# A routed-expert stage with 17 tiles of 256 slots and 6 of 128 in place of 23 tiles of 256

## The chip, the cores and the metric

The kernel runs on one core of a Trainium2 chip. The metric is the device time of the whole program in microseconds (us), the median of several runs. Engines are named as in the profile: PE is TensorE (matmuls), PEld its weight loads, DVE is VectorE, ACT is ScalarE, POOL is GpSimd, SP is SyncE, which here only issues transfers.

## What is computed

A decoder layer on x of 4 x 512 rows of 512 numbers: a gated recurrence, a cross attention, and a block of self attention and experts, with a layer norm behind each of the three. The change touches only the experts. There are 8 routed experts of inner width 352 and a shared expert of inner width 1408; each of the 2048 rows goes to the two routed experts with the largest router probability:

```python
top_w, top_i = jax.lax.top_k(probabilities, 2)        # of 8 experts, for each row
g = jnp.einsum('th,ehi->eti', h, w_gate_e)            # 512 -> 352
u = jnp.einsum('th,ehi->eti', h, w_up_e)              # 512 -> 352
y = jnp.einsum('eti,eih->eth', jax.nn.silu(g) * u, w_down_e)
routed = jnp.einsum('eth,te->th', y, combine)         # combine: the two weights of a row
sh = jax.nn.silu(h @ w_sh_gate) * (h @ w_sh_up) @ w_sh_down
x = x + routed + sh * jax.nn.sigmoid(h @ w_sh_eg)
```

## The kernel before

The last part of the program, moe (from L1959), runs as a list of passes (schedule, L1946): 12 passes of the shared expert (six parts of its width, two row groups each), then 23 passes of the routed experts, one for each tile, then 12 more of the shared expert. A tile (class Pass, L1936) is TW = 256 places for rows of one expert; there are NTILES = 23 of them, enough for any split of the 4096 pairs of row and expert. Which expert a tile belongs to is found on the chip: places (in the VectorE block) counts the rows of each expert, gives every pair of row and expert a slot, and fills the row numbers up_row and dn_row with which GpSimd later picks an expert's weights by indirect transfers.

Every product is made of three matmuls with the operands split into a high and a low part (product3, L132). In a routed tile the weights are stationary (128 of the 352 inner columns at a time, the last chunk has 96) and 256 rows move: three chunks, each 12 matmuls for gate and 12 for up. So the activation comes out with the inner width on the partitions, as the down product needs it. The down product (down, L2504) makes 128 rows at a time: the activation is stationary, 512 output columns move, 9 matmuls.

TensorE's order in a routed pass p is: gate and up of chunk 0; the down product of pass p - 1; gate of chunk 1; the turning of the next tile's rows (turn, L2482: 8 transposes from hs); up of chunk 1; chunk 2. The wait for the low parts of the rows (s_tlo) stands ahead of each pass, and the wait for the loaded rows (s_hs) in turn. ScalarE takes the sigmoid (L2233), the high part of the activation (L2240), the high parts of the next tile's gate and up weights (split_up, L2194, two of 128 x 1408), the high parts of the next tile's rows (high_rows, L2214), the high part of this tile's down weights (split_down, L2203) and the results (L2259). VectorE does the gating (L2293, L2296) and the low parts of all of them (L2278, L2282, L2301, L2400).

The raw weights have one landing buffer each (up_raw, dn_raw): GpSimd issues the transfer for the next tile (pick_up L2153, pick_down L2161) when VectorE has split the last. The split gate and up weights have two buffers, the rows hs two, the results ys four. SyncE works through one list: for each tile it issues the load of the rows of the tile after next (load_rows, L2082), then waits for and issues the stores of this tile's results (store_rows, L2088). So a load of rows stands behind the stores of the tile two before it, and these wait for ScalarE's results.

## Time and profile before

| what | us |
| --- | --- |
| median of 3 runs (2492.18 to 2497.55) | 2493.06 |
| the profiled execution | 2495.78 |
| its span | 2494.1 |
| TensorE busy in the span | 2374.0 |
| VectorE busy | 1353.1 |
| ScalarE busy | 1351.2 |
| GpSimd busy | 927.6 |

The span is what the profile's times count from and cover; the profiled execution's own time is 1.7 us longer. The routed passes lie between about 1976 and 2290 us of the span. In the views an instruction is given with the line of the kernel, what it writes and what it reads; matmuls overlap, so the duration of a single one is longer than their distance, and the chain of waits, which gives each matmul the time by which it moved the end, is the place to read a matmul's price.

### The profile page before, as it was taken

How to read it: one execution, taken by the hardware profiler on the slowest of the kernel's cores; microseconds unless marked ns; L12 is line 12 of the kernel's file. 1: busy time of each engine (PE TensorE's matmuls, PEld its weight loads, DVE VectorE, ACT ScalarE, POOL GpSimd, SP SyncE). 2: the span in 40 equal slices, each digit the busy share in tenths (PEclk: the TensorE clock that was granted, in tenths of full speed). 3: DMA queues.
4: the chain of work that ended last, by engine and by line, in shares of the span. 5: the costliest groups of instructions: out<-in, count | busy, mean ns of one | idle time of the engine just before them, and what ended most of it. 6: DMA issues, size and time to landing. Idle time of an engine off the chain costs nothing. (4 is left out here: it accounts for less than half of the span.)

```text
span 2494.1 us, 39149 instructions
## 1 busy us (share of the span) xinstructions
PE 2374.0 (95%) x15376; PEld 1537.8 (62%) x15376; DVE 1353.1 (54%) x2105; ACT 1351.2 (54%) x1714; POOL 927.6 (37%) x610
## 2 busy tenths in 40 slices
PE   8999899999999999999998899998899999999997
PEld 6877444444444444444334556565588899999885
DVE  6676534434443434443413755555565677776785
ACT  4332577677766777667995443433422366665221
POOL 1237654565465535654212433332033021221320
PEclk9999899999999999999999999999899999999999
DMA  6003774667455764756745000001144277775430
GB/s 219 17 18 106 221 197 117 157 167 194 118 146 158 196 170 97 186 155 167 191 87 203 18 1 18 1 18 54 60 163 160 92 238 243 243 237 185 144 119 34
DMA packets 206935, 331.46 MB, mean 133 GB/s; under 512 B 71264, under 2 KB 125792, under 8 KB 206560
## 3 DMA queue, kind: packets, MB, share of 16 engines
q1 hardware_dynamic: 188256, 252.80, 35.8%
q0 software_dynamic: 16336, 72.23, 8.8%
q10 hardware_dynamic: 2160, 3.93, 0.5%
q8 instruction: 122, 2.00, 0.3%
q14 instruction: 61, 0.50, 0.1%
HBM read 241.53 MB, written 99.42 MB: 137 GB/s over the span
## 5 line engine op out<-in xcount | busy, mean ns | idle before, releaser
L1052 ACT ACTIVATE A_c_prob<-c_psum 128x1024 f32<-128x1024 f32 x832 | 786.8, 1029 | 277.4 <-PE c_psum L1302 271.3
L982 POOL TENSOR_TENSOR E_c_roots<-E_c_roots,c_half 128x32 f32<-128x32 f32 (+1 forms) x70 | 363.3, 5191 | 406.6 <-DVE E_c_roots L1069 406.5
L1311 PE MATMUL c_psum<-A_c_prob,c_vq 128*17 128x512 f32 x3328 | 415.4, 599 | 8.6 <-DVE c_oT L1204 8.3
L137 PE MATMUL c_psum<-E_c_w,E_c_c 128*128 128x512 f32 x1248 | 313.8, 401 | 3.1 <-DVEq L1189 2.2
L1302 PE MATMUL c_psum<-c_qq,c_kq 64*128 64x512 f32 x1664 | 287.9, 438 | 18.8 <-ACT A_c_prob L1052 11.3
L137 PEld LDWEIGHTS c_psum<-E_c_w,E_c_c 128*128 128x128 f32 x1248 | 227.4, 188 | 124.6 <-issue 41.0
L1302 PEld LDWEIGHTS c_psum<-c_qq,c_kq 64*128 64x128 f32 x1664 | 136.6, 185 | 167.2 <-ACT A_c_prob L1052 91.4
L1108 DVE COPY E_c_unit<-c_psum 128x256 f32<-128x256 f32 x89 | 37.8, 425 | 327.8 <-PE c_psum L137 327.8
L2504 PE MATMUL m_psum<-A_m_dn_hi,A_m_a 128*128 128x512 f32 (+1 forms) x628 | 204.3, 394 | 2.2 <-DVE A_m_a L2301 2.2
L137 PE MATMUL m_psum<-R_m_t,m_up_hi 128*128 128x256 f32 (+1 forms) x1104 | 200.0, 283 | 0.0
L1311 PEld LDWEIGHTS c_psum<-A_c_prob,c_vq 128*17 128x17 f32 x3328 | 68.6, 96 | 188.4 <-issue 163.7
L1742 DVE TENSOR_REDUCE s_topx<-s_psum 128x4 f32<-128x2048 f32 (+1 forms) x64 | 95.5, 1492 | 146.2 <-PE s_psum L1860 137.0
L137 PEld LDWEIGHTS m_psum<-R_m_t,m_up_hi 128*128 128x128 f32 (+1 forms) x1104 | 165.8, 179 | 2.1
L2240 ACT ACTIVATE A_m_a<-Q_m_work 128x256 fp32r<-128x256 f32 (+2 forms) x113 | 56.7, 502 | 200.9 <-DVE Q_m_work L2296 159.2
L137 PE MATMUL m_psum<-R_m_t,m_up_lo 128*128 128x256 f32 (+1 forms) x552 | 154.7, 280 | 0.0
L1653 ACT ACTIVATE A_s_pT<-s_psum 128x2048 f32<-128x2048 f32 (+1 forms) x64 | 79.5, 1242 | 121.2 <-PE s_psum L1874 120.9
L2504 PEld LDWEIGHTS m_psum<-A_m_dn_hi,A_m_a 128*128 128x128 f32 (+1 forms) x628 | 117.8, 188 | 28.6 <-DVE A_m_a L2301 2.7
L137 PE MATMUL r_psum<-E_x,E_w_hi 128*128 128x512 f32 x384 | 121.0, 397 | 10.0 <-DVE E_w_lo L414 9.2
L2233 ACT ACTIVATE Q_m_work<-m_psum 128x256 f32<-128x256 f32 (+2 forms) x113 | 51.9, 459 | 134.2 <-PE m_psum L137 134.2
L2504 PE MATMUL m_psum<-Q_m_dn_lo,A_m_a 128*128 128x512 f32 (+1 forms) x314 | 123.1, 392 | 0.0
L975 POOL TENSOR_TENSOR E_c_c<-E_c_raw,E_c_c 128x512 fp32r<-128x512 f32 x89 | 118.7, 1333 | 7.1
L137 PE MATMUL m_psum<-R_g_hi,m_up_hi 128*128 128x512 f32 x264 | 105.6, 400 | 3.6 <-DVE m_up_lo L2278 3.6
(316 smaller groups left out, 4216.7 us busy)
## 6 DMA issues: line engine op xcount, KB each, us to landing
c_kq<-kd SPq DMA_DIRECT2D x248, 208.0 KB, 6.1
kd<-S_c_t SPq DMA_DIRECT2D x96, 256.0 KB, 4.0
E_c_raw<-in_ctxT SPq DMA_DIRECT2D x89, 256.0 KB, 4.2
qd<-A_c_q SPq DMA_DIRECT2D x64, 256.0 KB
c_qq<-qd SPq DMA_DIRECT2D x64, 256.0 KB, 3.1
vd<-A_c_vt SPq DMA_DIRECT2D x104, 136.0 KB, 3.0
c_vq<-vd SPq DMA_DIRECT2D x31, 442.0 KB, 9.0
R_m_hs<-slots SPq DMA_DIRECT2D x23, 512.0 KB
```

The costliest lines, as they stand in the source:

```text
L137: mm = pe.matmul(out, a(c), b(c), start=first and i == 0, stop=last and i == len(terms) - 1)
L975: pool.tensor_tensor(c_lo[:, job % 2], c_raw[:, n % CB], c_hi[:, job % 2], ALU.subtract).then_inc(s_clo, 1)
L982: pool.tensor_tensor(rr[:, unit % RB, 0:n], ms[:, unit % RB, 0:n], half[:, 0:n], ALU.pow).then_inc(s_r, 1)
L1052: act.activation(prob[:, t % PB, 2 * (u % 2):2 * (u % 2) + 2, :], score_banks[u % 3], ACT.Exp, scale=XD ** -0.5).then_inc(s_ex, 1)
L1108: dve.tensor_copy(raw[:, unit % RB, at:at + HD], src[:, 0:HD]).then_inc(s_k, 1)
L1302: mm = pe.matmul(score_banks[u % 3][:, s, :], kq[rows, q % 2, u % 2, kt * P:(kt + 1) * P], qq[rows, q % 2, u % 2, :], start=True, stop=True)
L1311: mm = pe.matmul(o_bank[32 * j:32 * j + VW, :], vq[:, q % 2, kt, j, :], prob[:, t % PB, j, :], start=kt == 0, stop=kt == CT - 1)
L1653: act.activation(pT[:, kt % 2, :, 0:L], psum[:, 0:HPC, 0:L], ACT.Exp, scale=SCALE).then_inc(s_ex, 1)
L1742: dve.reduce_max(topx[:, t, ::SD], psum[:, 0:HPC, 0:(t + 1) * P], AX_X).then_inc(s_top, 1)
L2233: act.activation(sig[0:rows, 0:width], gu_bank[n % 2][0][0:rows, 0:width], ACT.Sigmoid).then_inc(s_sig, 1)
L2240: act.activation(a_hi[0:rows, p % 2, i, 0:width], act_f[0:rows, 0:width], ACT.Copy).then_inc(s_ahi, 1)
L2504: mm = pe.matmul(y_bank[t], a[0:rows, p % 2, i, ts], w[0:rows, i, :], start=k == 0, stop=k == 3 * len(x.chunks) - 1)
```

## The change

Six of the 23 tiles become tiles of 128 slots; their places in the order are after the 3rd, 6th, 9th, 12th, 15th and 17th tile of 256 (ORDER). An expert's rows are cut into as many tiles of 256 as they fill by more than half of the last, and its last 128 or fewer go to a short tile; if the short tiles are used up or not needed, tiles of 256 or empty ones stand in, which places works out with a longer list of small VectorE operations. In a short tile (Pass.turned) the rows are stationary and the weights move, 352 columns at a time: 12 matmuls for gate and 12 for up. The activation then has the rows on the partitions, so three transposes on TensorE turn it, into the bank in which the gate product was, and ScalarE and VectorE take its high and low part from there. TensorE's order in a short tile is: gate; turn of the next tile's rows; up; the down product of the pass before; the three transposes. ScalarE's is: sigmoid, first weight split, rows, second weight split, down weights, results of the pass before, turned activation. VectorE's is: first half of the gating, first weight split, second half, second weight split, rows, down weights, low part of the turned activation. Loads, stores and turns of a short tile handle one block of 128 rows in place of two.

```diff
-NTILES = (B * T * 2 - NEXP) // TW + NEXP
-SLOTS = NTILES * TW
+PAIRS, SINGLES = 17, 6
+HALVES = 2 * PAIRS + SINGLES
+NTILES = PAIRS + SINGLES
+SLOTS = HALVES * P
+
+
+def order_of_tiles():
+
+    out, pair = [], 0
+    for single in range(SINGLES):
+        upto = min(3 * single + 3, PAIRS)
+        out += [*range(pair, upto), PAIRS + single]
+        pair = upto
+    return out
+
+
+ORDER = order_of_tiles()
+first_half = lambda column: 2 * column if column < PAIRS else column + PAIRS
...
-        self.subs = TT if self.shared else TW // P
-        self.chunks = [(i * P, P) for i in range(CHUNKS[unit_of(stage)])] if self.shared else IT
+        self.subs = TT if self.shared else 1 + (ORDER[tile] < PAIRS)
+        self.width = self.subs * P
+        self.turned = self.subs == 1
+        self.inner = [(i * P, P) for i in range(CHUNKS[unit_of(stage)])] if self.shared else IT
+        self.chunks = [(0, P)] if self.turned else self.inner
+        self.across = MI if self.turned else self.width
...
-                rows = slots[tile * TW:(tile + 1) * TW].rearrange("(s p) n -> p s n", p=P)
-                sp.dma_start(hs[:, tile % 2], rows).then_inc(s_hs[tile % 2], 16)
+                at, subs = first_half(ORDER[tile]), passes[R0 + tile].subs
+                rows = slots[at * P:(at + subs) * P].rearrange("(s p) n -> p s n", p=P)
+                sp.dma_start(hs[:, tile % 2, 0:subs], rows).then_inc(s_hs[tile % 2], 16)
 
             def store_rows(tile):
-                for s in range(TW // P):
-                    n = tile * (TW // P) + s
+                for s in range(passes[R0 + tile].subs):
+                    n, at = esub(R0 + tile) + s, first_half(ORDER[tile]) + s
                     sp.wait_ge(s_ye, n + 1)
-                    sp.dma_start(yslots[n * P:(n + 1) * P], ys[:, n % NY]).then_inc(s_ys[n % NY], 16)
+                    sp.dma_start(yslots[at * P:(at + 1) * P], ys[:, n % NY]).then_inc(s_ys[n % NY], 16)
...
+                def high_turned():
+                    act.wait_ge(s_turned, turned_before(p) + 1)
+                    act.wait_ge(s_y, ysub(p - 1))
+                    act.activation(a_hi[:, p % 2, :, 0:P], gu_bank[base(p) % 2][0][:, 0:NI * P].rearrange("p (i n) -> p i n", i=NI), ACT.Copy).then_inc(s_ahi, 1)
...
+                if x.turned:
+                    sigmoid(0)
+                    split_up(w + 1, 0)
+                    if not passes[p + 1].shared:
+                        high_rows(passes[p + 1].tile)
+                    split_up(w + 1, 1)
+                    split_down(w)
+                    results()
+                    high_turned()
+                    continue
...
+            def low_turned(x):
+                n = base(x.p)
+                dve.wait_ge(s_ahi, n + 1)
+                dve.tensor_tensor(a_lo[:, x.p % 2, :, 0:P], gu_bank[n % 2][0][:, 0:NI * P].rearrange("p (i n) -> p i n", i=NI),
+                                  a_hi[:, x.p % 2, :, 0:P], ALU.subtract).then_inc(s_alo, 1)
...
-                own.done(dve.tensor_reduce(many[:], few, AX_X, ALU.add))
+                each = lambda ap: ap.unsqueeze(2).to_broadcast([P, NEXP, NTILE])
+                per_tile = lambda ap: ap.unsqueeze(1).to_broadcast([P, NTILES, NEXP])
+                halves = count_f[:].unsqueeze(2).to_broadcast([P, NTILES, NEXP])
+                placed = by_expert(place[:])
+                behind = few_f
+                own.done(dve.tensor_scalar(below, ranks_f[:, 0:NEXP], -float(NEXP), None, ALU.add))
+                own.done(dve.tensor_reduce(np_e, few[:, :, 1::2], AX_X, ALU.add))
+                own.done(dve.tensor_reduce(ns_e, few[:, :, 0::2], AX_X, ALU.add))
                 own.wait()
-                own.done(dve.tensor_tensor_scan(upto_e[:], ones[:, 0:NEXP], many[:], 0.0, ALU.mult, ALU.add))
+                own.done(dve.tensor_tensor(ns_e, ns_e, np_e, ALU.subtract))
+                own.done(dve.tensor_tensor_scan(pairs_e, ones[:, 0:NEXP], np_e, 0.0, ALU.mult, ALU.add))
                 own.wait()
-                own.done(dve.tensor_tensor(many[:], upto_e[:], many[:], ALU.subtract))
+                own.done(dve.tensor_tensor_scan(singles_e, ones[:, 0:NEXP], ns_e, 0.0, ALU.mult, ALU.add))
+                own.done(dve.tensor_tensor(pair_at, pairs_e, np_e, ALU.subtract))
                 own.wait()
-                own.done(dve.scalar_tensor_tensor(by_expert(place[:]), many[:].unsqueeze(2).to_broadcast([P, NEXP, NTILE]), float(TW), by_expert(place[:]), ALU.mult, ALU.add))
-                own.done(dve.tensor_tensor(compared, upto_e[:].unsqueeze(1).to_broadcast([P, NTILES, NEXP]),
-                                           count_f[:].unsqueeze(2).to_broadcast([P, NTILES, NEXP]), ALU.is_le))
+                pairs = pairs_e[:, NEXP - 1:NEXP]
+                own.done(dve.scalar_tensor_tensor(turn_e, singles_e, pairs, ns_e, ALU.add, ALU.subtract))
+                own.wait()
+                own.done(dve.tensor_scalar(single_at, turn_e, float(PAIRS), pairs, ALU.min, ALU.max))
+                own.wait()
+                own.done(dve.tensor_tensor(single_at, single_at, turn_e, ALU.add))
+                own.wait()
+                own.done(dve.scalar_tensor_tensor(shift, pairs_e, -2.0, single_at, ALU.mult, ALU.add))
+                own.done(dve.scalar_tensor_tensor(by_expert(behind), each(np_e), float(TW), placed, ALU.mult, ALU.is_le))
+                own.done(dve.tensor_tensor(ns_e, ns_e, below, ALU.mult))
+                own.wait()
+                own.done(dve.tensor_tensor(by_expert(behind), by_expert(behind), each(shift), ALU.mult))
+                own.done(dve.scalar_tensor_tensor(placed, each(pair_at), float(TW), placed, ALU.mult, ALU.add))
+                own.done(dve.scalar_tensor_tensor(compared, per_tile(pairs_e), 2.0, halves, ALU.mult, ALU.is_le))
+                own.done(dve.tensor_tensor(matched, per_tile(single_at), halves, ALU.is_equal))
+                own.wait()
+                own.done(dve.scalar_tensor_tensor(place[:], behind, float(P), place[:], ALU.mult, ALU.add))
+                own.done(dve.tensor_tensor(matched, matched, per_tile(ns_e), ALU.mult))
+                own.wait()
+                own.done(dve.tensor_tensor(compared, compared, matched, ALU.add))
...
+                if x.turned:
+                    gated(x, 0, 0)
+                    split_up(w + 1, 0)
+                    gated(x, 0, 1)
+                    split_up(w + 1, 1)
+                    if not passes[p + 1].shared:
+                        low_rows(passes[p + 1].tile)
+                    split_down(w)
+                    low_turned(x)
+                    continue
...
+                if x.turned:
+                    n = base(p)
+                    pe.wait_ge(s_a, n - 1)
+                    for j in range(2):
+                        product3(pe, gu_bank[n % 2][j][:, 0:MI], lambda c: hi[:, c, 0:P], lambda c: lo[:, c, 0:P],
+                                 lambda c: up_hi[:, w % 2, j, c, :], lambda c: up_lo[:, w % 2, j, c, :], KC).then_inc(s_gu, 1)
+                        if j == 0 and not passes[p + 1].shared:
+                            turn(passes[p + 1].tile)
+                    down(passes[p - 1])
+                    pe.wait_ge(s_a, n + 1)
+                    for i in range(NI):
+                        mm = pe.transpose(gu_bank[n % 2][0][:, i * P:(i + 1) * P], act_f[:, i * P:(i + 1) * P], ident[:])
+                    mm.then_inc(s_turned, 1)
+                    continue
...
                         pe.wait_ge(s_a, n - 1)
+                        if n - 2 in turned_chunks:
+                            pe.wait_ge(s_alo, n - 1)
```

The rest gives the short tiles their widths and counts in the same functions, issues one more iota, and takes the buffers of the new small operations from places that are free at that time.

## Rows read from the trace of the kernel before

**Rows 1.** View by windows, twenty routed tiles (us, then each engine's busy us, PEclk, DMA share, GB/s)

```profile
2000.73:2273.52 272.79, 272.79 (x1962) 257.04 (x1962) 201.35 (x320) 173.33 (x301) 55.24 (x58) 1.00 0.71 241
```

**Rows 2.** Chain of waits in order of time: start us, us, what, how many

```profile
2081.67 0.88 PE m_psum L2482 x8
2082.55 7.10 PE m_psum L137 x60
2089.65 4.24 PE m_psum L2504 x18
...
2300.22 11.14 PE m_psum L137 x48
```

**Rows 3.** Timeline of ScalarE, one routed pass and a shared one: start us, us, instruction

```profile
1808.00 0.58 ACT L2233 ACTIVATE Q_m_work<-m_psum 128x512 f32<-128x512 f32 x1
...
2102.49 0.36 ACT L2233 ACTIVATE Q_m_work<-m_psum 128x256 f32<-128x256 f32 x1
2102.75 1.37 ACT L2194 ACTIVATE m_up_hi<-S_up_raw 128x1408 fp32r<-128x1408 f32 x1
...
2105.63 0.58 ACT L2259 ACTIVATE R_m_ys<-m_psum 128x512 f32<-128x512 f32 x1
...
2109.50 1.57 ACT L2214 ACTIVATE R_m_t<-m_psum,S_w 128x256 fp32r<-128x256 f32 x4
2110.94 1.51 ACT L2203 ACTIVATE A_m_dn_hi<-Q_m_dn_raw 128x1536 fp32r<-128x1536 f32 x1
```

**Rows 4.** Timeline of VectorE in the same routed pass

```profile
2103.13 0.42 DVE L2293 TENSOR_TENSOR Q_m_work<-m_psum,Q_m_work 128x256 f32<-128x256 f32 x1
...
2104.16 1.62 DVE L2278 TENSOR_TENSOR m_up_lo<-S_up_raw,m_up_hi 128x1408 fp32r<-128x1408 f32 x1 [0.15 <-ACT m_up_hi L2194]
...
2110.37 1.66 DVE L2400 SCALAR_TENSOR_TENSOR R_m_t<-m_psum,S_w,R_m_t 128x256 fp32r<-128x256 f32 x4 [2.67 <-ACT R_m_t L2214]
...
2112.74 1.75 DVE L2282 TENSOR_TENSOR Q_m_dn_lo<-Q_m_dn_raw,A_m_dn_hi 128x1536 fp32r<-128x1536 f32 x1
```

**Rows 5.** Timeline of SyncE's queue in a routed pass

```profile
2092.60 2.27 SPq L2088 DMA_DIRECT2D yslots<-R_m_ys  x2
...
2094.91 0.43 SPq L2082 DMA_DIRECT2D R_m_hs<-slots  x1
```

**Rows 6.** DMA view, 2101-2102, 2102-2103: packets, MB, share; then landing of seven stores

```profile
q1 hardware_dynamic: 57, 0.10, 27.1%
...
q1 hardware_dynamic: 8, 0.01, 3.7%
...
DMA to landing us min/median/max: 4.2/4.7/5.4
```

**Rows 7.** View by windows, while weights, results and rows are all under way

```profile
2093.50:2100.45 6.95, 6.95 (x60) 6.91 (x59) 4.27 (x8) 4.62 (x9) 0.94 (x1) 1.00 0.94 312
```

**Rows 8.** View by windows, two stops of TensorE, the second with what follows it

```profile
210.13:212.33 2.20, 0.00 (x1) 0.01 (x1) 0.00 (x0) 0.60 (x1) 0.41 (x4) 1.00 0.00 0
213.70:217.20 3.50, 3.50 (x12) 2.72 (x11) 0.10 (x1) 0.51 (x1) 3.50 (x1) 0.51 0.76 285
226.03:231.00 4.97, 3.38 (x17) 2.57 (x16) 4.87 (x10) 2.98 (x4) 4.74 (x1) 1.00 0.26 88
```

**Rows 9.** Timelines around places, TensorE's chain there, and GpSimd's later wait

```profile
1814.59 0.21 DVE L2354 TENSOR_REDUCE m_many<-S_m_equal 128x8 f32<-128x64 f32 x1
...
1818.74 0.18 DVE L2380 CAST m_slot<-S_m_slot 128x32 int32<-128x32 f32 x1
...
1826.16 0.69 DVE L2296 TENSOR_TENSOR Q_m_work<-Q_m_work,m_psum 128x512 f32<-128x512 f32 x1 [1.17 <-PE m_psum L137]
1827.55 0.69 DVE L2301 TENSOR_TENSOR A_m_a<-Q_m_work,A_m_a 128x512 fp32r<-128x512 f32 x1 [0.70 <-ACT A_m_a L2240]
...
1831.62 5.48 PE m_psum L2504 x24
...
1950.52 1.15 POOL L2153 DMA_INDIRECT S_up_raw<-in_up,m_up_row  x1 [30.93 <-DVE m_up_lo L2278]
```

More of the change, by code:

```diff
@@ L1972, in moe @@
     base = lambda p: sum(len(x.chunks) for x in passes[:p])
+    turned_before = lambda p: sum(x.turned for x in passes[:p])
+    turned_chunks = {base(x.p) for x in passes if x.turned}
     routed = lambda w: unit_of(w) is None
@@ L2020, in moe @@
         rank = S.tile("m_rank", at_s + NEXP * NTILE, NTILE, NEXP)
-        many = m.sb("many", [P, NEXP])
-        upto_e = m.sb("upto_e", [P, NEXP])
+        np_e, ns_e, pairs_e, singles_e, pair_at, turn_e, single_at, shift, below = (restart[:, i * NEXP:(i + 1) * NEXP] for i in range(9))
         picked = m.sb("picked", [P, NTILE, NEXP])
@@ L2224, in _ @@
                 p, w = x.p, x.stage
-                width = T if x.shared else TW
+                width = x.across
                 prev = passes[p - 1] if p else None
@@ L2240, in high_act, with results @@
                     act.activation(a_hi[0:rows, p % 2, i, 0:width], act_f[0:rows, 0:width], ACT.Copy).then_inc(s_ahi, 1)
+                def high_turned():
+                    act.wait_ge(s_turned, turned_before(p) + 1)
+                    act.wait_ge(s_y, ysub(p - 1))
+                    act.activation(a_hi[:, p % 2, :, 0:P], gu_bank[base(p) % 2][0][:, 0:NI * P].rearrange("p (i n) -> p i n", i=NI), ACT.Copy).then_inc(s_ahi, 1)
+                def results():
+                    for s in range(prev.subs):
+                        n = esub(p - 1) + s
+                        act.wait_ge(s_y, ysub(p - 1) + s + 1)
+                        if n >= NY:
+                            act.wait_ge(s_ys[n % NY], 16 * (n // NY))
+                        act.activation(ys[:, n % NY], y_bank[s], ACT.Copy).then_inc(s_ye, 1)
                 fresh = first[w] == p and w + 1 < stages
                 single = len(x.chunks) == 1
+                if x.turned:
[8 more added lines that the diff above has]
+                    continue
                 sigmoid(0)
@@ L2253, in _ @@
                 if prev and not prev.shared:
-                    for s in range(prev.subs):
-                        n = esub(p - 1) + s
-                        act.wait_ge(s_y, ysub(p - 1) + s + 1)
-                        if n >= NY:
-                            act.wait_ge(s_ys[n % NY], 16 * (n // NY))
-                        act.activation(ys[:, n % NY], y_bank[s], ACT.Copy).then_inc(s_ye, 1)
+                    results()
                 if first[w] == p and w and x.shared:
@@ L2285, in _, with gated @@
                 split_up(0, j)
-            def gated(x, i):
-                n, rows, width = base(x.p) + i, x.chunks[i][1], T if x.shared else TW
-                dve.wait_ge(s_sig, n + 1)
-                if n:
-                    dve.wait_ge(s_alo, n)
-                    dve.wait_ge(s_ahi, n)
-                dve.tensor_tensor(act_f[0:rows, 0:width], gu_bank[n % 2][0][0:rows, 0:width], sig[0:rows, 0:width], ALU.mult).then_inc(s_t1, 1)
+            def gated(x, i, half=None):
+                n, rows, width = base(x.p) + i, x.chunks[i][1], x.across
+                if half != 1:
+                    dve.wait_ge(s_sig, n + 1)
+                    if n:
+                        dve.wait_ge(s_alo, n)
+                        dve.wait_ge(s_ahi, n)
+                    dve.tensor_tensor(act_f[0:rows, 0:width], gu_bank[n % 2][0][0:rows, 0:width], sig[0:rows, 0:width], ALU.mult).then_inc(s_t1, 1)
+                if half == 0:
+                    return
                 dve.wait_ge(s_t1, n + 1)
@@ L2332, in _ @@
             own.done(dve.tensor_copy(part_f[:], part_i[:]))
+            own.done(dve.tensor_copy(ranks_f[:], ranks_i))
             by_expert = lambda ap: ap.rearrange("p (e t) -> p e t", e=NEXP)
@@ L2339, in _ @@
             total = by_expert(upto[:])[:, :, NTILE - 1]
-            few = equal_f[:, 0:NEXP * NEXP].rearrange("p (e k) -> p e k", e=NEXP)
-            start = count_f[:, 0:NEXP].unsqueeze(1).to_broadcast([P, NEXP, NEXP])
-            own.done(dve.scalar_tensor_tensor(few, start, float(TW), total.unsqueeze(2).to_broadcast([P, NEXP, NEXP]), ALU.mult, ALU.is_lt))
+            few = few_f.rearrange("p (e k) -> p e k", e=NEXP)
+            start = ranks_f[:].unsqueeze(1).to_broadcast([P, NEXP, 2 * NEXP])
+            own.done(dve.scalar_tensor_tensor(few, start, float(P), total.unsqueeze(2).to_broadcast([P, NEXP, 2 * NEXP]), ALU.mult, ALU.is_lt))
             own.wait()
@@ L2480, in turn @@
                 for k in range(KC):
-                    for s in range(TW // P):
+                    for s in range(passes[R0 + tile].subs):
                         tr = pe.transpose(t_bank[k // 2][:, (k % 2) * TW + s * P:(k % 2) * TW + (s + 1) * P],
@@ L2501, in down @@
                     k = 0
-                    for i, (r0, rows) in enumerate(x.chunks):
+                    for i, (r0, rows) in enumerate(x.inner):
                         for a, w in ((a_hi, dn_hi), (a_hi, dn_lo), (a_lo, dn_hi)):
-                            mm = pe.matmul(y_bank[t], a[0:rows, p % 2, i, ts], w[0:rows, i, :], start=k == 0, stop=k == 3 * len(x.chunks) - 1)
+                            mm = pe.matmul(y_bank[t], a[0:rows, p % 2, i, ts], w[0:rows, i, :], start=k == 0, stop=k == 3 * len(x.inner) - 1)
                             k += 1
```

40 lines of the change are left out of this document (24 added, 16 removed).

## The prediction

> **What bounds the kernel now.** I first read the stage of the routed experts in the view by windows: over twenty tiles TensorE is busy for all 272.79 us, at full granted clock, while VectorE is busy for 201 us, ScalarE for 173 us, and the transfers take 0.71 of the sixteen DMA engines at 241 GB/s [rows 1]. So TensorE alone sets the pace, 272.79/20 = 13.64 us a tile, and the other engines and the queues have room. Then the chain of waits: in this stage it never leaves TensorE, so what a tile costs is the sum of its matmuls [rows 2]. Last the timelines of ScalarE, VectorE and the queues inside one tile, since a tile of half the rows still brings a whole expert's weights: its splits (ScalarE, VectorE) and its transfers do not halve [rows 3 to 6].
>
> **The gain on TensorE.** From the chain: 60 matmuls with 256 moving columns take 7.10 us, 0.1183 each; 18 with 512 take 4.24, 0.2356 each; 48 of the gate and up form with 512 take 11.14, 0.232 each; 8 transposes take 0.88, 0.109 each [rows 2]. A tile of 256 is 72 x 0.1183 + 18 x 0.2356 + 8 x 0.109 = 13.64 us. A tile of 128 has 24 gate and up matmuls with 352 moving columns, 9 of the down product, 4 transposes of rows and 3 of the activation. No row has 352 columns: the bounds are 0.118 (256) and 0.232 (512); I take the line between them, 0.161, which gives 3.86 us, and keep 2.84 and 5.57 for the range. Sum: 3.86 + 2.12 + 0.44 + 0.33 = 6.75 us. The change makes six tiles of 256 into six of 128, so 6 x (13.64 - 6.75) = 41.3 us, if TensorE stays as full as it is.
>
> **What a short tile asks of the others.** I count from S, the start of its gate product; each step is one row's duration. TensorE: gate 1.93; turning the next tile's rows 0.87, to 2.80; up 1.93, to 4.74; the down product of the pair before, 4.24, to 8.98; three transposes, to 9.30, where the next pair begins. ScalarE: sigmoid at 1.93 (0.45, between 0.36 for 256 and 0.58 for 512), first weight split 1.37 to 3.8, rows 1.57 to 5.4, second split 1.37 to 6.7; then the split of the down weights, which waits for the down product at 8.98 and ends at 10.5; two results of 0.58 to 11.7; the turned activation, about 0.52, to 12.2 [rows 3]. VectorE: first half of the gating to 3.0, split of 1.62 to 5.4, second half to 5.9, split from 6.7 to 8.4, low parts of the rows 1.66 to 10.0, down weights 1.75 from 10.5 to 12.3, low part of the activation to 12.8 [rows 4].
>
> First wait: the next pair's gate needs those low rows, ready at 10.0, and TensorE is there at 9.30: 0.7 us. The low activation at 12.8 is then just in time, for after its first chunk (2.84) TensorE asks for it at 12.84. The transposes of the activation wait for the second gating, 5.9, and find it done 3 us before.
>
> Second wait, the rows turned inside the short tile. Their load is issued 2094.91 - 2086.81 = 8.1 us after the pair before began (2086.81 is 2089.65 less the 2.84 of the first chunk [rows 2, 5]). That pair lasts 13.64 - 0.44 = 13.20, and the turn comes 1.93 later: 7.0 us after the issue. Where only pairs follow each other it is 13.64 + 2.84 + 4.24 + 1.42 - 8.1 = 14.0 us. In the trace this load still moves 0.10 MB between 2101 and 2102, and its last packets go by 2103, so it lands 7.1 to 8 us after its issue [rows 6]: a wait from 0 to 1 us, most of which only takes the place of the first. Together 0.9 us for each short tile with a pair behind it, five of the six.
>
> Third wait, the largest: the rows for the pair behind that. SyncE issues them after it has stored the two results of the pair before (the load stands 2.3 us behind the first store [rows 5]), and those results now stand behind the down weights on ScalarE. So the issue is at about 11.7 + 0.4 = 12.1. TensorE wants them after first chunk (10.2 to 13.0), down product 2.12 and one gate chunk 1.42: at 16.6, 4.5 us after the issue. Lower bound: a store of half that size lands in 4.2 to 5.4 us [rows 6], so no wait to 0.9. Upper bound: 8 us, as the same load may take above, a wait of 3.5. Between them by bytes: two stores and the rows, 1.05 MB, and the down weights of the next tile, 0.79 MB, at the 312 GB/s of the stretch in which the transfers were full [rows 7] take 5.9 us. I take 6.5 from issue to landing, nearest to the same load's 7.1: a wait of 2.0 us, five times.
>
> The Trainium skill (DMA: Bandwidth & Descriptors, Anatomy of one DMA — SWDGE (gpsimd) path) fits a transfer as 2.0 us plus its bytes at 436 GB/s; by that, an estimate, 0.52 MB land in 3.2 us, the third wait is gone, and the sum is that of the first rival below. The trace does not agree, with 7.1 us for the same bytes beside other transfers; the fit is for transfers that GpSimd issues.
>
> The clock. Early in the run TensorE stood for 2.20 us and then ran 3.50 us at a granted clock of 0.51, that is at 1.2 GHz; after another stop, of 4.97 - 3.38 = 1.6 us, the clock stayed at 1.00 [rows 8]. A wait of 2.0 us lies between. One fall costs about half of 3.5 us, 1.75; I take half of five falls, 4.4 us, and keep 0 and 8.8. The Trainium skill (TensorE: Matmul & The Clock Gate, Why this matters for your kernels) says that matmuls with few rows make the clock swing down at each wait for data; the first row agrees, the second does not.
>
> Hidden edits. places() grows by about 15 small operations on VectorE, some 3.8 us by the present spacing (17 operations from 1814.59 to 1818.92, 0.25 each [rows 9]). VectorE idles for 1.17 us behind it, and the low activation of that pass ends at 1828.2 where TensorE wants it at 1831.62 [rows 9]: cover of 3.4 + 1.2 us, so nothing, as long as it grows by less than 4.5 us; beyond that it costs one for one. Scattering the rows on GpSimd begins as much later; it stands for 30.9 us behind that work, with nothing to do, before it loads the second tile's weights [rows 9]. The shorter buffers, the two iotas and the changed order of columns cost nothing on the path. The last short tile has a shared pass behind it, whose first chunk is twice as long, and no rows to turn: no wait.
>
> Sum: 41.3 - 5 x 0.9 - 5 x 2.0 - 4.4 = 22.4 us. Against the profiled execution's 2495.78 us that is 2473.4; this execution lies 2.7 us above the median of the runs, so in their terms 2471. I say 2472.
>
> **Rivals.** (1) The rows land in time. For it: the queues are busy for only 0.71 of the stage, and the stores land in 4.7 us. Against it: 7.1 us for this very load. Then 41.3 - 5 x 0.7 = 37.8 us, 2455. (2) The waits are longer and each brings the clock down: rows 8 us after the issue (3.5 us), 0.9 before, a fall of 1.75: 6.2 x 5 = 31 us, leaving 10, 2483; for it, that the 0.79 MB of down weights start in the same moment. (3) Slower: the transfers become the bound. A tile moves 0.241 x 13.64 = 3.29 MB now; a short one 2.77 (128 rows less in and out), since the 2.2 MB of an expert's weights stay, by their shapes. Three pairs and a short tile move 12.64 MB, and four tiles took 54.6 us: if the queues carry less than 232 GB/s over this cycle it is slower than before, because the weights have one landing buffer each and the next load waits for VectorE's split of the last. At 220 GB/s the cycle takes 57.5 us: 5 x 2.9 less the 7 us of the last short tile, 7 us slower, 2500. Against it: 241 GB/s were carried at a share of 0.71. (4) The waits eat the gain, 8 us for each short tile: no change. (5) The wide matmul costs as 512 columns do: 10 us less gain, 2482; as 256 do: 6 us more.
>
> **How the numbers follow.** Forecast, with the wide matmul's bounds, 0.45; (1) 0.20; (2) 0.17; (4) 0.08; (3) 0.10. A measurement of this kernel tells about 0.2%, 5 us, from no change. Faster: 0.45 + 0.20 + 0.17 = 0.82; same 0.08; slower 0.10. The range goes from (1), 2455, to 2489, where (2) ends with a wide matmul that costs more.
>
> **What would show it.** In the profile after: gate and up matmuls with 352 columns 0.16 us apart; after each of five short tiles a wait of TensorE at the transposes of the rows (line of turn) of about 2 us, and under 1 us ahead of the next gate; the short tile's stretch at 9.3 us and the pair behind it at 11.5 plus the waits; two or three stretches of 0.5 granted clock behind the waits. If the wait for rows is missing, (1) holds; if TensorE waits at the gate for weight splits, (3). The forecast is wrong above all if the landing time of the rows is not 6 to 8 us.

## The result, and the profile after

| | before | after |
| --- | --- | --- |
| median, us (4 runs each) | 2495.31 (2492.18 to 2499.41) | 2466.41 (2465.14 to 2468.81) |
| ratio, 95% interval | | 0.9886 [0.9872, 0.9900] |
| the profiled execution | 2495.78 | 2465.14 |
| its span | 2494.1 | 2463.4 |
| expert stage: from the first expert matmul to where the chain of waits leaves TensorE | 671.1 | 641.6 |

The change makes the kernel 28.9 us faster; 2472 was forecast, with a range from 2455 to 2489. In the two profiled executions 30.7 us lie between the spans. The last row of the table has 29.4 of them; 2.0 more were there before the first expert matmul (at 1795.32 before, at 1793.34 after), where nothing was changed, and 0.7 are given back behind the point (2466.39 and 2434.98) where the chain leaves TensorE. The last matmuls of the shared expert stand behind that point, beside the layer norm of the rows that are done. So 29.4 us is what the prediction's sum must answer to.

The page of the profile after, span and busy time of each engine:

```profile
span 2463.4 us, 38351 instructions
...
PE 2334.0 (95%) x15028; PEld 1497.9 (61%) x15028; DVE 1341.3 (54%) x2085; ACT 1336.9 (54%) x1684; POOL 925.5 (38%) x612
```

TensorE is busy for 40 us less than before, near the 41.3 us of the sum, and some 10 us came back as idle time. The view by windows of after shows where (columns as in [rows 1]): the shared passes ahead of the routed ones, the routed passes, and the 7 us behind the longest stop:

```profile
1793.34:1990.00 196.66, 196.66 (x889) 161.66 (x890) 125.03 (x204) 54.31 (x81) 49.36 (x57) 0.99 0.41 136
1990.00:2261.18 271.18, 261.34 (x1805) 243.11 (x1805) 202.94 (x314) 173.59 (x295) 59.00 (x62) 1.00 0.72 244
...
2019.81:2026.90 7.09, 7.09 (x40) 6.28 (x41) 5.33 (x7) 2.99 (x6) 1.88 (x2) 1.00 0.45 156
```

Ahead of the routed passes TensorE never stops, so the longer places costs nothing. In the routed passes it is idle for 9.8 us (9.7 without two pauses under 0.1), at full granted clock, where before it was never idle [rows 1]. The transfers carry 244 GB/s, hardly more than before. The waits of TensorE in the routed passes of after (us in total, times, longest):

```profile
PE m_psum L2576 <- DMA R_m_hs<-slots: 6.5, 5, 1.6
PE m_psum L2598 <- DVE A_m_a L2356: 2.9, 4, 0.7
PE m_psum L137 <- DVE R_m_t L2484: 0.3, 1, 0.3
```

Four of the five waits for rows (1.61, 1.26, 1.40 and 0.86 us) are inside a short tile, at the turn; each has a wait of 0.72 for the low part of the turned activation behind it. The fourth short tile does not wait for its rows. There TensorE waits 0.34 us for the low rows ahead of the pair behind, and the fifth wait for rows, 1.32 us, is at the turn inside that pair. The chain of waits of after, from inside a pair to the end of the last short tile:

```profile
2248.61 8.10 PE m_psum L137 x60
2256.70 4.15 PE m_psum L2598 x18
2260.85 0.33 PE m_psum L2623 x3
```

The 60 matmuls of the first line are 36 of the pair with 256 moving columns and 24 of the short tile with 352: (8.10 - 36 x 0.1183) / 24 = 0.160 us each. Then come the down product of the pair and the three transposes of the activation, at the prices that the sum had for them.

The timeline of after around the first short tile, SyncE's loads of rows (SPq) and TensorE's stops (in square brackets the idle time and what ended it):

```profile
2011.17 0.43 SPq L2108 DMA_DIRECT2D R_m_hs<-slots  x1
...
2019.81 1.07 PE L2576 MATMUL m_psum<-ident,R_m_hs 128*128 128x128 f32 x8 [1.61 <-DMA R_m_hs<-slots]
...
2029.98 0.46 SPq L2108 DMA_DIRECT2D R_m_hs<-slots  x1
...
2030.84 0.50 PE L2598 MATMUL m_psum<-A_m_dn_hi,A_m_a 128*128 128x512 f32 x1 [0.72 <-DVE A_m_a L2356]
...
2034.45 1.04 PE L2576 MATMUL m_psum<-ident,R_m_hs 128*128 128x128 f32 x8
```

The first load takes 8.6 us to the turn and TensorE waits for it. The second is wanted 4.5 us after its issue, as the prediction had it, and it is there. The view of transfers says why; of each stretch, packets, MB and share of the 16 engines for the queue of SyncE (q1) and that of GpSimd's weights (q0), then KB and us to landing of the load of rows, first for 2011.2 to 2019.8, then for 2030.0 to 2032.5:

```profile
q0 software_dynamic: 343, 1.79, 59.4%
q1 hardware_dynamic: 416, 0.79, 24.3%
...
R_m_hs<-slots SPq DMA_DIRECT2D x1, 512.0 KB, 8.5
...
q1 hardware_dynamic: 387, 0.73, 90.9%
...
R_m_hs<-slots SPq DMA_DIRECT2D x1, 512.0 KB, 3.9
```

The same 512 KB land in 8.5 us beside weights and in 3.9 us with SyncE's own stores alone.

### The profile page after: what moved, and what is told of

The parts are those of the page before. It is cut to its first block and busy times, and to the rows that moved or that the text cites. A ratio compares the mean times of both kernels' runs of the same rounds, so it can differ in the third digit from the quotient of the medians.

```text
span 2463.4 us, 38351 instructions
## 1 busy us (share of the span) xinstructions
PE 2334.0 (95%) x15028; PEld 1497.9 (61%) x15028; DVE 1341.3 (54%) x2085; ACT 1336.9 (54%) x1684; POOL 925.5 (38%) x612
## 5 line engine op out<-in xcount | busy, mean ns | idle before, releaser
L137 PE MATMUL c_psum<-E_c_w,E_c_c 128*128 128x512 f32 x1248 | 312.6, 400 | 3.0 <-DVEq L1189 2.2
L137 PEld LDWEIGHTS c_psum<-E_c_w,E_c_c 128*128 128x128 f32 x1248 | 226.6, 188 | 124.5 <-issue 41.0
L2598 PE MATMUL m_psum<-A_m_dn_hi,A_m_a 128*128 128x512 f32 (+1 forms) x592 | 193.8, 396 | 5.3 <-DVE A_m_a L2356 2.9
L2269 ACT ACTIVATE A_m_a<-Q_m_work 128x512 fp32r<-128x512 f32 (+2 forms) x95 | 49.1, 517 | 187.3 <-DVE Q_m_work L2346 186.8
L137 PE MATMUL m_psum<-R_m_t,m_up_hi 128*128 128x256 f32 (+1 forms) x816 | 148.7, 283 | 0.3 <-DVE R_m_t L2484 0.3
L2598 PEld LDWEIGHTS m_psum<-A_m_dn_hi,A_m_a 128*128 128x128 f32 (+1 forms) x592 | 111.8, 189 | 31.4 <-DVE A_m_a L2356 4.0
L137 PE MATMUL r_psum<-E_x,E_w_hi 128*128 128x512 f32 x384 | 120.2, 394 | 11.2 <-DVE E_w_lo L414 9.5
L137 PEld LDWEIGHTS m_psum<-R_m_t,m_up_hi 128*128 128x128 f32 (+1 forms) x816 | 122.6, 179 | 2.2 <-DVE R_m_t L2484 0.6
L2598 PE MATMUL m_psum<-Q_m_dn_lo,A_m_a 128*128 128x512 f32 (+1 forms) x296 | 116.5, 394 | 0.0
L2262 ACT ACTIVATE Q_m_work<-m_psum 128x512 f32<-128x512 f32 (+3 forms) x101 | 48.2, 478 | 123.6 <-PE m_psum L137 123.6
L137 PE MATMUL m_psum<-R_m_t,m_up_lo 128*128 128x256 f32 (+1 forms) x408 | 114.4, 280 | 0.0
L137 PE MATMUL m_psum<-R_g_hi,m_up_hi 128*128 128x512 f32 x264 | 105.6, 400 | 3.7 <-DVE m_up_lo L2325 3.7
```

What stands on the lines that cost most here:

```text
L137: mm = pe.matmul(out, a(c), b(c), start=first and i == 0, stop=last and i == len(terms) - 1)
L2262: act.activation(sig[0:rows, 0:width], gu_bank[n % 2][0][0:rows, 0:width], ACT.Sigmoid).then_inc(s_sig, 1)
L2269: act.activation(a_hi[0:rows, p % 2, i, 0:width], act_f[0:rows, 0:width], ACT.Copy).then_inc(s_ahi, 1)
L2598: mm = pe.matmul(y_bank[t], a[0:rows, p % 2, i, ts], w[0:rows, i, :], start=k == 0, stop=k == 3 * len(x.inner) - 1)
```

## The experiments

The theory after these views: what is left of TensorE's idle time comes from the place of the loads of rows in SyncE's list, and not from the weights or from too little bandwidth; and the stop inside the short tile hides the one predicted for the pair behind it. The rivals put it on the weights, the splits or the transfers; each expectation states its own. "Stage" is the time from the first expert matmul to where the chain of waits leaves TensorE, "idle" the idle time of TensorE in the routed passes, both in the profiled execution. The kernel before was run beside each of them; the ratio is to that.

| kernel | median, us | ratio, 95% interval | idle, us | stage, us |
| --- | --- | --- | --- | --- |
| before | 2495.31 | 1 | 0 | 671.1 |
| after | 2466.41 | 0.9886 [0.9872, 0.9900] | 9.7 | 641.6 |
| e1_rows_early | 2463.01 | 0.9884 [0.9867, 0.9900] | 5.6 | 637.2 |
| e2_rows_early_short | 2482.64 | 0.9955 [0.9940, 0.9970] | 14.8 | 649.8 |
| e3_turn_mid | 2472.84 | 0.9915 [0.9898, 0.9931] | 13.9 | 648.5 |
| e4_unturned | 2473.47 | 0.9919 [0.9902, 0.9936] | 0 | 648.9 |
| e5_rows_two | 2457.15 | 0.9849 [0.9827, 0.9871] | 2.6 | 633.8 |
| e6_rows_two_low | 2464.17 | 0.9877 [0.9856, 0.9897] | 2.6 | 633.8 |
| e7_in_a_row | 2487.10 | 0.9962 [0.9949, 0.9974] | 21.4 | 662.1 |
| e8_rows_two_again | 2456.59 | 0.9852 [0.9834, 0.9870] | 2.6 | 633.5 |
| e9_rows_two_low_mid | 2462.63 | 0.9873 [0.9856, 0.9889] | 4.2 | 636.1 |

**e1_rows_early: every load of rows one place earlier in SyncE's list.**

```diff
-            load_rows(0)
-            load_rows(1)
+            for tile in range(3):
+                load_rows(tile)
             for tile in range(NTILES):
-                if tile + 2 < NTILES:
-                    load_rows(tile + 2)
-                else:
+                if tile + 3 < NTILES:
+                    load_rows(tile + 3)
+                if tile + 2 >= NTILES:
```

> Only the order of the transfers that SyncE issues is changed: each load of rows stands one tile earlier, ahead of the stores behind which it waited. Theory (the rows come too late because their load is issued too late): the waits of TensorE at the turning of rows, 6.5 us in five short tiles, fall to 0; with each goes about 0.16 us of refilling; the wait for the low activation (0.72 us, four times) turns into one of 0.2 to 0.6 for the low rows. The time falls from 2466.4 by about 7, to 2459. Rival (the queues are full, so an earlier load of rows only pushes the weights back): the wait moves to the weight splits and the time stays at 2465 to 2468.

The waits of TensorE in the routed passes of e1:

```profile
PE m_psum L2598 <- DVE A_m_a L2351: 3.0, 3, 1.6
PE m_psum L137 <- DVE R_m_t L2484: 2.6, 5, 0.5
```

No wait for rows is left; the five waits of 0.52 us for the low rows are the prediction's first wait. But a new one stands in three of the pairs behind a short tile. In the timeline of e1 around the longest of them, SyncE's load of rows stands 0.7 us ahead of GpSimd's load of the down weights, whose split on ScalarE then waits:

```profile
2127.31 0.97 SPq L2108 DMA_DIRECT2D R_m_hs<-slots  x1
...
2128.01 0.94 POOL L2189 DMA_INDIRECT Q_m_dn_raw<-in_dn,m_dn_row  x1 [3.21 <-DVE Q_m_dn_lo L2329]
...
2136.04 1.49 ACT L2231 ACTIVATE A_m_dn_hi<-Q_m_dn_raw 128x1536 fp32r<-128x1536 f32 x1 [1.91 <-DMA Q_m_dn_raw<-in_dn,m_dn_row]
```

The down weights take 8.0 us to arrive, and the rows beside them 7.6. In after a load of rows stands just as close ahead of the down weights, but it goes out 4.6 us behind the last load of gate and up weights and lands in 4.0; here only 3.45 us lie between. So the theory holds for the rows and the rival for what comes then: the wait moves to the next transfer that shares the engines with a load of rows. e5, below, leaves that load in its old place, and this wait is gone. The idle time falls by 4.1 us and the stage by 4.4; the ratios can't be told apart.

**e2_rows_early_short: only the rows of the tile right behind a short one are loaded earlier.** This takes away the stop inside the short tile and nothing else.

```diff
                 if tile + 2 < NTILES:
-                    load_rows(tile + 2)
+                    if not passes[R0 + tile + 1].turned:
+                        load_rows(tile + 2)
+                    if tile + 3 < NTILES and passes[R0 + tile + 2].turned:
+                        load_rows(tile + 3)
```

> Only the load of the rows that are turned inside a short tile is issued one tile earlier; the load behind it stays. Theory A (the wait in the short tile gives the next load its time, so the third wait of the prediction is only hidden): the wait in the short tile goes, and one of about 1.3 us, as the fourth short tile has it now, comes at the turn in the pair behind each of five short tiles: 6.6 us, the time stays at 2466. Theory B (the third wait was an accident of the fourth tile): it shows once at most and the time falls by 5 to 6, to 2461.

The waits for rows of e2, all five of them at the turn in the pair behind a short tile (0.31, 4.00, 3.09, 2.43 and 2.39 us):

```profile
PE m_psum L2579 <- DMA R_m_hs<-slots: 12.2, 5, 4.0
```

The view of transfers of e2, 2087 to 2089, inside the wait of 4.00 us, and the landing of the load that ends it, issued at 2082.27:

```profile
q0 software_dynamic: 92, 0.48, 63.8%
q1 hardware_dynamic: 105, 0.19, 29.1%
...
R_m_hs<-slots SPq DMA_DIRECT2D x1, 512.0 KB, 8.6
```

How far the load stands behind the last load of gate and up weights, in after (its rows go out at 2029.98) and in e2:

```profile
2025.30 0.94 POOL L2181 DMA_INDIRECT S_up_raw<-in_up,m_up_row  x1 [2.47 <-DVE m_up_lo L2325]
...
2078.82 0.94 POOL L2184 DMA_INDIRECT S_up_raw<-in_up,m_up_row  x1 [1.79 <-DVE m_up_lo L2328]
...
2082.27 0.87 SPq L2108 DMA_DIRECT2D R_m_hs<-slots  x1
```

And its windows: the wait of 4.00 us and what follows it, what follows that of 3.09 us, then the wait of 2.43 us and what follows:

```profile
2086.99:2090.99 4.00, 0.00 (x0) 0.03 (x1) 0.61 (x1) 0.38 (x1) 0.94 (x1) 0.88 0.97 302
2091.00:2097.80 6.80, 6.80 (x36) 6.80 (x37) 4.20 (x8) 3.60 (x7) 0.00 (x0) 0.57 0.59 229
2145.40:2149.00 3.60, 3.60 (x21) 3.60 (x22) 1.60 (x5) 2.47 (x5) 0.00 (x0) 0.63 0.96 357
2195.22:2197.65 2.43, 0.00 (x1) 0.03 (x1) 0.61 (x1) 0.38 (x1) 0.94 (x1) 1.00 0.93 360
2197.70:2204.00 6.30, 6.30 (x55) 6.30 (x56) 4.62 (x9) 3.64 (x7) 0.36 (x1) 1.00 0.79 301
```

With one wait less the kernel is 0.7% slower, 16.2 us in the medians. Of this the profiled execution shows 8.2 us in the stage; 6.3 more of its time lie before the first expert matmul (1799.60 against 1793.34), where nothing was changed, and the other executions have no trace. Theory A had the place right and the size too small (6.6 us). This is the third wait of the prediction, 12.2/5 = 2.4 us on the mean, and the fall of the clock behind it (0.57 behind the wait of 4.00 us, 0.63 in a stretch behind that of 3.09). In after it was masked: where TensorE stopped inside the short tile, the next load of rows went out 4.6 to 4.7 us behind the last load of gate and up weights and landed in 3.9 to 4.1. Without that stop it went out 3.45 to 3.6 us behind them in e2, and landed in 4.9, 8.6, 7.7, 7.0 and 6.8 us; in the fourth short tile of after these were 3.9 and 5.6 us. The stop let the weights arrive first, so that the next rows had the engines to themselves.

**e3_turn_mid: the three transposes of the activation stand between the two halves of the down product before, and its high and low part ahead of the down weights.**

```diff
-                    split_down(w)
-                    results()
                     high_turned()
+                    split_down(w)
+                    results()
...
-                    split_down(w)
                     low_turned(x)
+                    split_down(w)
...
-                    down(passes[p - 1])
-                    pe.wait_ge(s_a, n + 1)
...
+                    down(passes[p - 1], turn_activation)
```

> The three transposes of the activation are moved between the two halves of the down product of the pair before, and ScalarE and VectorE take the turned activation ahead of the down weights. Theory (the wait of 0.72 us in four tiles is for the low activation, last in VectorE's order): it goes or falls to 0.2, with its refilling, the time falls by 3, to 2463. Rival (the low part of the down weights, which then stands last, is as late): no change, 2466.

The waits of TensorE in the routed passes of e3:

```profile
PE m_psum L2576 <- DMA R_m_hs<-slots: 8.1, 6, 3.1
PE m_psum L2598 <- DVE A_m_a L2351: 2.9, 4, 1.4
PE m_psum L2598 <- issue: 2.5, 4, 0.6
```

The 0.72 us of the activation are replaced by 0.63 for the low part of the down weights (last line), for both come from VectorE one behind the other and TensorE needs both. The split of the down weights stands later, so their next load does, and four pairs wait for it (second line). The first wait for rows grows to 3.1 us, and the granted clock falls behind it, to 0.58 in this window of e3:

```profile
2024.00:2027.40 3.40, 3.40 (x16) 3.40 (x17) 0.24 (x1) 2.30 (x5) 0.94 (x1) 0.58 0.36 88
```

The expected gain was not there, and the kernel is 6 us slower than after.

**e4_unturned: the short tiles stay, but in the old form.** Weights stationary, 128 rows moving, nothing to turn.

```diff
-        self.turned = self.subs == 1
+        self.turned = False
```

> The short tiles stay, but with the weights stationary and 128 rows moving, as the tiles of 256 have it: 72 gate and up matmuls of 128 columns in place of 24 of 352, nothing turned. If one costs 0.109, as a transpose of 128 columns does: 7.85 + 2.12 + 0.44 = 10.4 us for 6.75, 22 us more, of which some 10 come back since the waits have more time: 2478. If half of 256 columns, 0.059: 2466 or a little less. If it costs as 256 columns do, 0.118: 11.1 us, 26 us more, less 10, 2482. At a higher price than that (0.17 or more) all of the gain is gone, 2495.

TensorE does not stop once in the routed passes. The chain of waits of e4, a short tile between two pairs:

```profile
2015.26 6.91 PE m_psum L137 x60
...
2026.39 1.29 PE m_psum L137 x12
...
2028.58 6.23 PE m_psum L137 x60
```

With 128 moving columns the matmul costs 1.29/12 = 0.1075 us by the second line and (6.91 - 36 x 0.1183) / 24 = 0.110 by the first, against 0.1183 with 256. The chunk whose stationary operand has 96 columns costs less: (6.23 - 24 x 0.1183 - 12 x 0.1075) / 24 = 0.0875, since 24 of the last line's 60 matmuls are of the next pair. With 128 moving columns in both, the price thus goes with the columns of the stationary operand. A tile is 48 x 0.1075 + 24 x 0.0875 + 2.13 + 0.44 = 9.8 us; six would save 6 x (13.64 - 9.8) = 23 us, and the stage is 22.2 shorter than before. Halving the rows alone thus gives 22 of the 29 us; the turned form has 41.3 - 23 = 18 us more on TensorE and loses some 11 of them to waits (the 9.7 us of idle time and what each stop costs beside it, see below). The Trainium skill (TensorE: Matmul & The Clock Gate, LDWEIGHTS (loading the stationary operand)) gives its load a time of the number of its columns divided by 1.2, in ns: by that, an estimate, 107 and 80. The first agrees with this trace, the second is 7.5 ns short of it.

**e5_rows_two and e8_rows_two_again: the rows of the two tiles behind a short one are loaded earlier, all others stay.** Theory: this takes away both waits for rows and leaves the load of the down weights alone.

```diff
+            def issued_before(store):
+                early = lambda tile: tile < NTILES and any(passes[R0 + tile - k].turned for k in (1, 2) if tile >= k)
+                return [tile for tile in (store + 2, store + 3) if tile < NTILES and early(tile) == (tile == store + 3)]
...
-                if tile + 2 < NTILES:
-                    load_rows(tile + 2)
-                else:
+                for ahead_of in issued_before(tile):
+                    load_rows(ahead_of)
+                if tile + 2 >= NTILES:
```

> The rows of the two tiles behind a short tile are loaded one place earlier, all others in their old place. With every load earlier, TensorE still waited 3.0 us in three pairs behind a short tile, because the down weights landed 8 us after their issue beside a load of rows that now stood there. Theory (the order of the two kinds of load in the queues decides): that load is out of the way, the down weights land in 5 to 6 us, the waits are 0.52 us for the low rows at five places and under 1 us in all for the low activation; 3.5 us idle in place of 5.6; time 2461. Rival (the down weights are late in any order, since their buffer is single): the same waits, 2463.

The waits of TensorE in the routed passes of e5:

```profile
PE m_psum L137 <- DVE R_m_t L2488: 2.6, 5, 0.5
```

And its routed passes in the view by windows:

```profile
1990.00:2252.00 262.00, 259.41 (x1800) 242.41 (x1800) 202.89 (x315) 172.82 (x294) 58.83 (x62) 1.00 0.75 252
```

All that is left is the prediction's first wait, 0.52 us five times. The stage is 7.9 us shorter than that of after, for 7.1 us less idle time, and no split of the down weights waits any longer. This kernel beats after and e1. It was run again beside others:

> The kernel with the rows of two tiles loaded earlier, once more, beside the next one. Idle 2.6 us at five places; the same time as the first time, 2455 to 2459, if chance between runs is under 2 us.

It came out the same, with the same five waits.

**e6_rows_two_low: e5, and VectorE makes the low rows ahead of the second weight split.**

```diff
-                    split_up(w + 1, 1)
                     if not passes[p + 1].shared:
                         low_rows(passes[p + 1].tile)
+                    split_up(w + 1, 1)
```

> As the last, and in a short tile VectorE takes the low part of the next rows ahead of the second weight split. Theory: the wait of 0.52 us for the low rows falls to 0.1 to 0.2 at the weight split, which is then last, at 9.3 us after the start: 1.8 us less, 2459. Rival: the split is late by as much: 2461.

The waits of TensorE in the routed passes of e6:

```profile
PE m_psum L2602 <- DVE A_m_a L2360: 2.6, 5, 0.5
```

The same half microsecond now falls on the low activation: it goes with whatever VectorE makes last. The stage is as long as that of e5. The median is 7 us higher; in the profiled execution the stage has no such difference, and the other executions have no trace, so this stays open.

**e9_rows_two_low_mid: e6 with the transposes where e3 has them.**

```diff
+                    high_turned()
                     split_down(w)
                     results()
-                    high_turned()
...
-                    split_up(w + 1, 1)
                     if not passes[p + 1].shared:
                         low_rows(passes[p + 1].tile)
+                    split_up(w + 1, 1)
+                    low_turned(x)
                     split_down(w)
-                    low_turned(x)
...
+                    down(passes[p - 1], turn_activation)
```

> The rows of two tiles earlier, the low rows ahead of the second split, and the activation turned between the halves of the down product. With the low rows alone moved, the 0.51 us moved to the low activation. Theory (with the rows in time, only VectorE's order is left): the low activation comes before it is asked for; what is last is the low part of the down weights at 12.3 us, asked for at 12.1: 0.1 to 0.2 us at five places, 2 us less than the one above. Rival (moving the transposes cost 6 us before, and not only since its rows were late): no gain, or slower.

The waits of TensorE in the routed passes of e9:

```profile
PE m_psum L2602 <- issue: 2.3, 5, 0.5
PE m_psum L2602 <- DVE A_m_a L2355: 1.9, 3, 0.8
```

The half microsecond is there a third time (first line, 0.46 for the low part of the down weights), and the later split of the down weights costs 1.9 us more, as in e3. The last 2.6 us were not taken away by any order that was tried.

**e7_in_a_row: the six short tiles one after another, behind all pairs.** The theory was that the spacing carries the change: between short tiles the other engines and the queues catch up.

```diff
-    out, pair = [], 0
...
-    return out
+    return [*range(NTILES)]
...
                     pe.wait_ge(s_a, n - 1)
+                    if n - 2 in turned_chunks:
+                        pe.wait_ge(s_alo, n - 1)
```

> The six short tiles stand one behind the other at the end of the routed stage. Theory (transfers carry 312 GB/s at most when full): a short tile moves 2.75 MB, 8.8 us for 6.75 of TensorE, so about 2 us of waiting at each of five, 10 to 11 in all, as much as now: 2465 to 2469. Rival, the prediction's third (one landing buffer for each weight, so a load cannot start until VectorE has split the last): split 3 us, landing 5 to 8, issue 1 to 2, some 11 us a short tile: 5 x 4.5 = 22 us of waiting, 2476 or more, and the clock falls with it.

The chain of waits of e7, one turn from short tile to short tile, is no longer TensorE's alone:

```profile
2246.56 0.59 ACT R_m_ys L2277
2247.16 0.32 SPq L2109
2247.53 4.26 DMA R_m_hs<-slots
...
2251.93 0.73 PE m_psum L2571 x4
2252.66 3.38 PE m_psum L137 x12
2256.03 2.08 PE m_psum L2593 x9
```

And the whole row of short tiles, in the view by windows:

```profile
2200.00:2285.00 85.00, 63.56 (x321) 56.47 (x320) 50.81 (x70) 44.74 (x71) 14.99 (x16) 0.89 0.59 200
```

Most of the gain is gone: 21.4 us of idle time, 15.5 of it in five waits for rows, and a granted clock of 0.89. It is a loop: result on ScalarE, its store, the load of the next rows behind it in SyncE's list, the turn, the products, the next result. Next to next (2259.59 for the following result) that is 13.0 us, against 6.75 of work for TensorE. Part of it is the clock: the 12 matmuls of L137 take 3.38 us here, where 12 x 0.160 is 1.92. The transfers use 0.59 of their engines in the meantime, at 200 GB/s, and 312 GB/s is not the most that they carry: e2 has stretches with 357 and 360. So it is the order of the list and the landing time, not bandwidth, that bound a row of short tiles in this order of the list. Neither the theory's full queues nor the rival's late weights are in this chain, though the rival's 22 us of waiting and its fall of the clock came about. A row of short tiles with earlier loads was not run.

## Why the prediction was right, and where its sizes were off

**The gain on TensorE, 41.3 us: right.** The 352-column matmul costs 0.160 us, 0.161 was taken from the line between 256 and 512 columns. With the idle time the sum closes: 41.3 - 9.7 of stops - 10 x 0.16 is 30.0 us, and 29.4 were measured. The 0.16 is the overlap: a matmul's record lasts 0.32 us and the next begins 0.16 later, so a stop is taken to cost that much more than the idle time it shows; this is an estimate, from the 352-column form alone. The same sum gives 41.3 - 2.6 - 5 x 0.16 = 37.9 for e5, where the stage is 37.3 shorter.

**First and second wait, 0.9 us for each short tile: too small.** Measured are 2.33, 1.98, 2.12, 0.34 and 1.58 us for the five, 1.67 on the mean. The size of this term failed, and more in how its parts add than in the landing. The load was wanted 7.0 us after its issue and taken to land 7.1 to 8 us after it, as in before [rows 6]; in the five tiles it took 8.5, 8.2, 8.3, 6.9 and 7.8, and the one that landed inside 7.0 us is that of the fourth, which has no stop. But "most of which only takes the place of the first" and "just in time" for the low activation did not count that a late turn of the rows makes everything behind it on ScalarE and VectorE late: where the stop is, 0.72 us of waiting follow; where e5 takes the stop away, 0.52 for the low rows remain, near the 0.7 that the first wait was said to cost.

**Third wait, 2.0 us for each: the mechanism was right, the place wrong.** In after it appears once, with 1.32 us (0.26 on the mean of five). The moment when the rows are wanted, 4.5 us behind the issue, was met. The step that failed is the landing time of 6.5 us: it added the bytes of the next tile's down weights to the queue, and in after these came behind the rows, which landed in 3.9 us. e2 shows the term as it was meant: without the stop inside the short tile the rows land in 4.9 to 8.6 us, 7.0 on the mean, and TensorE waits 2.4 us on the mean, near the 6.5 and 2.0 of the prediction. The two waits were added up as if they were independent; the first, 1.26 to 1.61 us where it comes, shields the second. The fourth short tile of after says the same the other way round: no stop inside, then 1.32 us at the next turn.

Beside this stands what the prediction cited from the Trainium skill (DMA: Bandwidth & Descriptors, Anatomy of one DMA — SWDGE (gpsimd) path), an estimate of 3.2 us for these bytes, by a fit for transfers that GpSimd issues. The 3.9 us with nothing but SyncE's transfers are near it, and the 8.5 and 8.6 us beside the weights are not.

**The clock, 4.4 us: nothing in after.** Its stops in the routed passes are 1.61 us at most, and the granted clock is 1.00 there. In e2 and e3, where stops of 3.09 us and more occur, it falls as the prediction assumed; behind the two waits of e2 nearest to the assumed 2.0 us, 2.43 and 2.39, it stayed at 1.00. The term went with the third wait.

**The hidden edits: right.** TensorE is busy for all 196.66 us from the first shared pass to the routed ones, so places stayed under its cover, and the last short tile has no wait, as was said.

**The rivals.** (1), rows in time, was said to give 2455 and is e5, at 2457 and 2457: it needed the loads to be issued earlier. (2) needed waits of 3.5 us; single ones in e2 reach that. (3), the transfers as the bound, is not seen: the routed passes of e5 run at 252 GB/s, and in e7, the worst case for it, the queues are at 200 GB/s with engines to spare. (4) does not hold, and (5) is settled by the 0.160.

So the time was forecast with a sum of which the large term was right, and the losses came out as 11 us in place of 19, since two of them exclude each other. That the time lies only 6 us from the forecast is in part luck: the first and second wait took 8.4 us in place of 4.5, the third 1.3 in place of 10, and the clock nothing in place of 4.4. Of the signs that the prediction named, the 0.16 us came, but not the wait of about 2 us behind each short tile nor the stretches of low clock. e2, where the third wait comes as forecast, is 21.3 us shorter in its stage than before, near the sum's 22.4.

## What to carry to other kernels

When a tile is halved on the bound engine, list what is not halved, and look at the order in the queue that feeds the next tile: an issue that stands behind a store comes late by the whole chain that makes the result. Waits in a row are not added up; ask what the first lets arrive, and expect the next to show when the first is taken away (e2 took a wait away, and its stage is 8.2 us longer than that of after). Interleave the short tiles with long ones: the same six in a row lose most of the gain.

## What the runs showed of the hardware

- At a granted clock of 1.00 a matmul with a new stationary operand of 128 columns takes 0.1075 to 0.110 us with 128 moving columns (e4), 0.118 with 256, 0.160 with 352 (after) and 0.232 with 512 (before). From 256 to 128 moving columns half the columns bring less than a tenth; at 128, a stationary operand of 96 columns in place of 128 brings a fifth (0.0875, e4).
- A load of 512 KB landed in 3.9 us where its own queue was alone (after), in 8.5 us with the weights' queue at 59% of the DMA engines (after), and in 8.6 us with that queue at 64% in two of them (e2).
- The granted clock was unchanged behind stops of TensorE of 1.3 to 1.6 us (after), and behind two of 2.43 and 2.39 us (e2); it fell to the lower level behind 2.20 us early in before [rows 8], and behind 3.09 and 4.00 (e2) and 3.10 us (e3). Every run stops for 2.24 us (2.23 in e7) ahead of its last down product: behind it the granted clock stayed at 1.00 in before, e1, e5, e6 and e8, and was 0.77 or 0.78 in after, e2, e3, e4, e7 and e9, where these 24 matmuls took 7.3 us in place of 5.7. So between 2.2 and 2.4 us the length of a stop alone did not decide it.
